# A perceiver layer with 257 context rows: the last column of the probabilities comes to its rows by small DMAs in place of POOL, PE and DVE

## Time and profile before

| | us |
|---|---|
| median of 3 runs | 970.79 (970.17 to 971.96) |
| the profiled execution | 969.11 |
| its span, first to last instruction | 967.1 |
| PE busy | 943.9 |
| DVE busy | 613.0 |
| ACT busy | 607.3 |
| POOL busy | 373.8 |

### The profile page before, as it was taken

One profiled execution on the slowest core, in us unless ns is written; L12 is line 12 of the kernel. 1 busy time (PEld: TensorE's weight loads), 2 busy tenths in 40 slices (PEclk: granted clock), 3 DMA queues, 4 the chain that ended last, 5 costly groups with the idle time before them and its releaser, 6 DMA issues.

```text
span 967.1 us, 23520 instructions
## 1 busy us (share of the span) xinstructions
PE 943.9 (98%) x9012; PEld 783.6 (81%) x9012; DVE 613.0 (63%) x1286; ACT 607.3 (63%) x1487; POOL 373.8 (39%) x484
## 2 busy tenths in 40 slices
PE   9999999999999999999999999999999999999998
PEld 7767888787888878798887878888787888877775
DVE  4765858476685847668485666747567584746461
ACT  3545657667575766767576675757757566674533
POOL 1423534244352524435253352524326252433330
PEclk9999999999999999999999999999999999999999
DMA  8314231322323132132222313122222313222000
GB/s 304 120 51 124 59 105 49 100 81 65 105 78 90 51 101 81 60 110 61 88 69 87 95 60 94 60 87 89 81 80 81 90 49 89 87 73 72 9 12 22
DMA packets 58013, 79.03 MB, mean 82 GB/s; under 512 B 10288, under 2 KB 39856, under 8 KB 57904
## 3 DMA queue, kind: packets, MB, share of 16 engines
q1 hardware_dynamic: 56192, 76.38, 25.9%
q10 hardware_dynamic: 1712, 1.16, 0.4%
HBM read 73.05 MB, written 4.46 MB: 80 GB/s over the span
## 4 chain that ended last, share of the span: by engine, by line
PE 78%; DVE 9%; ACT 7%; issue 3%; POOL 1%; DMA 0%; DVEq 0%; POOLq 0%; ACTq 0%
PE gb L369 16%; PE scores L428 7%; PE acc L459 7%; PE gb L492 6%; PE acc L455 6%; PE scores L432 6%; PE ptp L442 5%; PE acc L460 5%; PE gb L613 3%; PE gb L602 3%; DVE xn L840 3%; ACT probs L685 3%; PE gb L401 3%; DVE probs L853 2%; DVE small L846 2%
## 5 line engine op out<-in xcount | busy, mean ns | idle before, releaser
L1100 POOL TENSOR_TENSOR t_l<-raw_t,t_h 128x516 fp32r<-128x516 f32 x128 | 167.5, 1309 | 193.6 <-PE scores L432 131.0
L685 ACT ACTIVATE probs<-scores,small 128x257 f32<-128x257 f32 x256 | 119.1, 471 | 134.6 <-DVE small L846 134.4
L846 DVE TENSOR_REDUCE small<-scores 128x2 f32<-128x514 f32 x128 | 88.3, 690 | 127.5 <-PE scores L432 127.4
L1109 POOL TENSOR_TENSOR ptm<-probs,head 128x32 f32<-128x32 f32 x128 | 35.1, 274 | 261.9 <-DVE probs L853 261.9
L853 DVE TENSOR_TENSOR probs<-probs,small 128x514 f32<-128x514 f32 x128 | 101.7, 794 | 4.4
L459 PE MATMUL acc<-pt,raw_n 128*128 128x256 f32 x256 | 89.6, 431 | 0.0
L442 PE MATMUL ptp<-ident,probs 128*128 128x128 f32 x512 | 78.7, 276 | 10.5 <-DVE probs L853 9.4
L696 ACT ACTIVATE pt<-ptp 128x512 f32<-128x512 f32 x128 | 77.2, 603 | 13.2 <-PE ptp L442 11.7
L455 PE MATMUL acc<-pt,raw_n 128*64 128x128 f32 x1024 | 82.7, 282 | 2.3 <-ACT pt L696 0.4
L428 PE MATMUL scores<-t_h,qk_h 128*128 128x258 f32 x256 | 83.3, 325 | 0.0
L455 PEld LDWEIGHTS acc<-pt,raw_n 128*64 128x64 f32 x1024 | 55.4, 136 | 31.9 <-issue 21.0
(11 more groups left out here) (178 smaller groups left out, 2768.8 us busy)
## 6 DMA issues: line engine op xcount, KB each, us to landing
raw_t<-in_ctx_t SPq DMA_DIRECT2D x128, 258.0 KB, 3.3
raw_n<-in_ctx_n SPq DMA_DIRECT2D x128, 192.0 KB, 2.4
xb<-in_x SPq DMA_DIRECT2D x16, 256.0 KB, 4.3
vsp<-tail_values SPq DMA_DIRECT2D x256, 2.0 KB
out<-ob SPq DMA_DIRECT2D x16, 256.0 KB, 2.9
xin<-in_x SPq DMA_DIRECT2D x15, 256.0 KB, 2.9
khat<-in_wq ACTq DMA_DIRECT2D x1, 512.0 KB, 4.3
wv<-in_wv SPq DMA_DIRECT2D x1, 512.0 KB, 6.3
```

The lines of the kernel that those rows point to most:

```text
L685: go(probs[n % 2][:, r, 0:L], scores[:, r, 0:L], ACT.Exp, bias=nmax[:, r:r + 1], accum_out=rsum[:, r:r + 1]).then_inc(s["exp_ready"], 1)
L846: v_.tensor_reduce(nmax[:], scores[:, :, 0:L], AX.X, ALU.max, negate=True)\
L1100: p_.tensor_tensor(t_l[m % 2][:], raw_t[m % RING][:], t_h[m % 2][:].bitcast(F32), ALU.subtract)\
```

## The change

The last column is copied by SP. For every batch two DMAs, one for each r, read one element from each of 128 partitions of `probs` and write 4 rows of 32 elements of `psp`, straight to the place where WV needs them. `psp` becomes two buffers, zeroed at the start by DVE (one more memset; the zeros of the second also feed PE's warm-up in place of ones). POOL's tail_column, PE's TP, DVE's psp item, `ptm` and the three tables with their loads are dropped. ACT's exponentials wait for the tail DMAs of n - 2, WV for those of all 8 batches. The values of the last row are loaded only into the half that is read: 8 DMAs a group and not 16. The new copy stands in SP's order at the head of each step, before load_t and load_n.

```diff
-         ["TP"]]
+         []]
...
-        ptm = [sb(f"ptm{i}", [P, 2, 2, G, H]) for i in range(2)]
-        psp = sb("psp", [P, G, S])
-        ones = psp[:].rearrange("p b s -> p (b s)")
+        psp = [sb(f"psp{i}", [P, G, S]) for i in range(2)]
+        zeros = psp[1][:].rearrange("p b s -> p (b s)")
...
                 for h in range(H):
                     cols = slice(h * DH, (h + 1) * DH)
-                    for half in range(2):
-                        sp.dma_start(vsp[half * 64 + h:half * 64 + 64:H, cols], scratch[g * G:(g + 1) * G, cols])\
-                            .then_inc(vsp_in, 16)
+                    half = h // 4
+                    sp.dma_start(vsp[half * 64 + h:half * 64 + 64:H, cols], scratch[g * G:(g + 1) * G, cols])\
+                        .then_inc(vsp_in, 16)
+
+            def tail_column(n):
+
+                g, b = n // G, n % G
+                if n == 0:
+                    sp.wait_ge(s["psp_ready"], 1)
+                sp.wait_ge(s["probs_ready"], n + 1)
+                if b == 0 and g > 1:
+                    bank, k = BANK["WV1", g - 2]
+                    sp.wait_ge(bank_filled[bank], k)
+                for r in range(2):
+                    row = 64 * r + H * b + 4 * r
+                    sp.dma_start(psp[g % 2][row:row + 4, b], probs[n % 2][:, r, L - 1:L]).then_inc(tail_in[n % 2], 16)
...
                     n = i * G + b
+                    if n < B:
+                        tail_column(n)
                     if n + RING + 1 < B:
                         load_t(n + RING + 1)
...
-                drained("TP", g)
-                pe.wait_ge(vsp_in, 256 * (g + 1))
+                for t_in in tail_in:
+                    pe.wait_ge(t_in, 16 * G * (g + 1))
+                pe.wait_ge(vsp_in, 128 * (g + 1))
...
                 if n > 1:
-                    act.wait_ge(s["ptm_ready"], n - 1)
+                    act.wait_ge(tail_in[n % 2], 32 * (n // 2))
...
-            GAPS = [[["psp-1"], ["S2-2", "S3-2"], ["WV0-1", "WV1-1"]],
+            GAPS = [[[], ["S2-2", "S3-2"], ["WV0-1", "WV1-1"]],
...
-            v_.memset(ones, 1.0).then_inc(s["ones_ready"], 1)
+            v_.memset(zeros, 0.0)
+            v_.memset(psp[0][:], 0.0).then_inc(s["psp_ready"], 1)
...
                     part(i, b, 0)
-                    if 0 <= n + 1 < B:
-                        tail_column(n + 1)
                     part(i, b, 1)
```

More of the change, by code:

```diff
@@ L65 @@
 TILES.update({"Sp": ["S0", "S1"], "Sq": ["S2", "S3"], "St": ["St0", "St1"]})
-SHIFT = {"XT": PREP, "TP": HERE}
+SHIFT = {"XT": PREP}
 SHIFT.update({f"q{p}": PREP for p in range(4)})
@@ L166, in build @@
         mask = sb("mask", [P, P], U8)
-        head = sb("head", [P, 2, 2, H])
-        same = sb("same", [P, G])
-        diag = sb("diag", [P, S])
         raw_t = [sb(f"raw_t{i}", [P, 2, LP]) for i in range(RING)]
@@ L250, in build @@
                              "out_done"))
+        tail_in = [sem(f"tail_in{i}") for i in range(2)]
         ctxt_in = [sem(f"ctxt_in{i}") for i in range(RING)]
@@ L254, in build @@
         bank_drained = [sem(f"bank_drained{i}") for i in range(BANKS)]
-        names = ("half_ready ones_ready zeros_ready small_ready scores_ready nmax_ready exp_ready probs_ready pt_ready ptev_ready "
-                 "acc_ready pc_ready ptm_ready var0_ready var1_ready var2_ready rstd0_ready rstd1_ready rstd2_ready xn0_ready xn1_ready xn2_ready high_act_ready high_pool_ready low_ready qk_h_ready xb_ready ob_ready "
+        names = ("half_ready psp_ready zeros_ready small_ready scores_ready nmax_ready exp_ready probs_ready pt_ready ptev_ready "
+                 "acc_ready pc_ready var0_ready var1_ready var2_ready rstd0_ready rstd1_ready rstd2_ready xn0_ready xn1_ready xn2_ready high_act_ready high_pool_ready low_ready qk_h_ready xb_ready ob_ready "
                  "wq_ready weights_ready wz_h_ready xt1_h_ready xt2_h_ready xt2_l_ready o_h_ready o2_h_ready tanh_ready dec_ready hat_ready rhat_ready dve_chain").split()
@@ L263, in build @@
         scratch = nc.dram_tensor("tail_values", [B, INNER], F32, kind="Internal").ap()
-        SMALL = [(mask_raw, a["mask"]), (bw_raw, a["bw"]), (head[:], a["head"]), (same[:], a["same"]),
-                 (diag[:], a["diag"]), (vecs[:, 0:2], a["ln_g"]), (vecs[:, 2:4], a["ln_b"]),
+        SMALL = [(mask_raw, a["mask"]), (bw_raw, a["bw"]),
+                 (vecs[:, 0:2], a["ln_g"]), (vecs[:, 2:4], a["ln_b"]),
                  (vecs[:, 6:14], a["b1"])]
@@ L477, in wz_product @@
                 done("WZ", 0, last)
[L479 to L485, removed]
             def wv(g):
@@ L501, in wv @@
                         rows_ = slice(64 * (h // 4), 64 * (h // 4) + 64)
-                        head(h, vsp[rows_, h * DH:(h + 1) * DH], psp[rows_].rearrange("p b s -> p (b s)"), start=i == 1)
+                        head(h, vsp[rows_, h * DH:(h + 1) * DH], psp[g % 2][rows_].rearrange("p b s -> p (b s)"), start=i == 1)
                     for h in pairs[i]:
@@ L623, in _ @@
             steps = {"WV": wv, "Y1": y1, "v": v, "O2": o2_, "Y2": y2, "Pf": pf_, "Qf": qf_, "Y3": y3,
-                     "TP": turn_tails, "VT": lambda g: tail_values(), "WZ": lambda g: wz_product()}
+                     "VT": lambda g: tail_values(), "WZ": lambda g: wz_product()}
             for n in ("XT", "XT2", "XT3"):
@@ L641, in stay_busy @@
                 for k in range(count):
-                    mm(ptp[:, 0], ones[:, 0:P], ones, start=True, stop=True)
-            pe.wait_ge(s["ones_ready"], 1)
+                    mm(ptp[:, 0], zeros[:, 0:P], zeros, start=True, stop=True)
+            pe.wait_ge(s["psp_ready"], 1)
             stay_busy(WARM)
@@ L705, in step @@
             def step(name, g):
-                if name in ("Y1", "Y2", "Y3", "TP", "Sp", "Sq"):
+                if name in ("Y1", "Y2", "Y3", "Sp", "Sq"):
                     return
@@ L922, in step @@
                     drain(n, g, v_.tensor_tensor(wz_l[:], t[:], wz_h[:].bitcast(F32), ALU.subtract))
[L923 to L927, removed]
                 elif n == "Y1":
@@ L1005, in _ @@
                     [[], ["S0-1", "S1-1"], ["xn0+2"]]]
-            AT_END = [[[["psp-1"], ["S2-2", "S3-2"], ["WV0-1", "WV1-1"]],
+            AT_END = [[[[], ["S2-2", "S3-2"], ["WV0-1", "WV1-1"]],
                        [[], [], ["Y1-1"]],
@@ L1101, in parts @@
                     .then_inc(s["low_ready"], 1)
[L1103 to L1111, removed]
             def hat(n, g):
@@ L1244 @@
     p = np.arange(P)
-    heads = 4 * np.arange(2)[None, :] + p[:, None] // S
-    head = np.repeat((heads[:, :, None] == np.arange(H))[:, :, None], 2, 2).astype(np.float32)
-    same = ((p[:, None] % 64) // H == np.arange(G)).astype(np.float32)
-    diag = (p[:, None] % S == np.arange(S)).astype(np.float32)
     def column(v):
@@ L1257 @@
         "x": np.ascontiguousarray(np.asarray(x).reshape(B * S, D)), "ctx_t": ctx_t, "ctx_n": ctx_n,
-        "ctx_tail": ctx_tail, "head": np.ascontiguousarray(head), "same": same, "diag": diag,
+        "ctx_tail": ctx_tail,
         "wq": chunks(np.asarray(L0_xattn_Wq)), "wk": wk, "wv": wv, "wo": chunks(np.asarray(L0_xattn_Wo)),
```

## The result

The changed kernel takes 991.37 us (median, 991.05 to 992.08), 1.0212 times as long as the kernel before (970.71 in the same comparison; 95% interval of the ratio 1.0194 to 1.023). That is 20.7 us slower, outside the range of 965.5 to 978.0. The sign was that of the forecast, the size was 4.6 times as large.

What follows compares the result with a forecast made beforehand. PE was taken to bound the kernel, with DVE's chain through the second LayerNorm setting the pace at batch 3. Terms -4.8 + 4.5 + 4.8 = +4.5 us on the median 970.8 gave 975.3 us, range 965.5 to 978.

Steps and rivals of the forecast that it cites:

- The sign: Whole kernel: slower, by a sum of +4.5 us; chance of slower 0.44.
- Elsewhere: POOL's earlier operations at batches 0, 4 and 7: the products have room (batch 4's over 2 us), so nothing added.
- TP: PE's stream: four instructions a group dropped, 0.37 us each group in 13 groups, -4.8 us.
- Batch 3: POOL's cast gets between xn1's two halves on DVE, delaying PE 0.30 us in 15 groups, +4.5 us.
- rival 2: DVE keeps its turn at xn1 and wins at batch 6; only TP's gain stays, 966.0 us; chance 0.17.
- Batch 6: POOL's k2 issues before DVE's product at line 853, delaying PE 0.34 us in 14 groups, +4.8 us.
- rival 1: Only batch 3 is hit, the product wins at batch 6: 970.5 us; chance 0.30.
- SP and the traffic: SP's queue and DMA engines: tail DMAs land in time, 32768 element packets at 71 ns have room; 0.
- Rival 4: SP: a tail DMA holds SP for 1.4 us, delaying the next group's exponentials; 977 to 982 us; chance 0.05.

Runs made afterwards that it cites:

- e1: The changed kernel with POOL's wait for the product kept where the tail column stood, the operation itself still dropped: 964.5 us, ratio 0.9933 to the kernel before.
- e3: The changed kernel with POOL's wait for the product in step b = 3 alone: 970.46 us, ratio 0.9999 to the kernel before.
- e12: e9 with two unused tensors, so that tensors allocated behind them lie at the addresses of the kernel before: 958.74 us, ratio 0.9884 to the kernel before.
- e5: The changed kernel with POOL's wait for the product in step b = 2 alone: 984.88 us, ratio 1.015 to the kernel before.
- e6: The changed kernel with POOL's wait for the product in step b = 5 alone: 988.78 us, ratio 1.018 to the kernel before.
- e8: e1 with 16 vsp DMAs a group again and not 8: 1001.94 us, ratio 1.0324 to the kernel before.
- e11: The changed kernel, POOL's t_l of batch 8g + 4 waiting for xn1 and cast of batch 8g + 6 for xn2: 958.61 us, ratio 0.9867 to before.
- e9: e1 with one wait more, POOL's t_l of batch 8g + 4 starting only when xn1 is written: 954.79 us, ratio 0.9842 to the kernel before.
- e2: The kernel before with POOL's tail column moved one step later, no small DMAs, TP kept: 980.16 us, ratio 1.0099 to the kernel before.

## Why the prediction was wrong

**The step that failed** is "*Elsewhere* there is room: ... batch 4's meets a t_l, but its product was ready over 2 us early". It asked whether POOL's earlier operations delay the product of batch 4, and whether PE's transposes feel that. They hardly do: in the changed kernel these transposes wait for 0.1 us in 13 groups together. But it didn't ask what else stands on DVE before that product (both halves of xn2), what stands behind it (Qa0's drain), and which tile of PE's needs the bank. And it saw one operation of POOL there, where three come: the cast in front of t_l meets line 912, and with the tail column gone xb follows t_l at once. That place costs 1.42 us a group against before and 1.46 against e1; times 15 groups 22 us, and e3 takes back 20.9.

The other terms, by their own steps:

- *TP, -4.8 us at 0.37 a group:* step 7 is 0.37 shorter than before, and in e12, at the old addresses, 0.36. Right. The product of the next group's batch 0 now takes 1.75 us, and its slack fell from 1.8 to 0.39 us, against some 0.3 foretold.
- *Batch 3, +4.5 at 0.30:* step 2 is 6.97 before and 7.27 after. Right. xn1's pair took 1.94 us in the place of 1.64, with the cast in between, as worked out:

```profile
490.24 1.30 POOL L1102 TENSOR_TENSOR t_l<-raw_t,t_h 128x516 fp32r<-128x516 f32 x1
491.49 0.68 POOL L1098 CAST t_h<-raw_t 128x516 fp32r<-128x516 f32 x1
...
490.38 1.94 DVE L846 TENSOR_SCALAR xn<-x,mv,rstd 128x256 f32<-128x256 f32 x2 [0.28 <-POOL rstd L1165]
```

  This rules out rival 2, by which DVE would keep its turn. Held back in e5, the cast gives back more than that, 6.2 us, since step 3 gets 0.11 us shorter as well. Why it does was not tried.
- *Batch 6, +4.8 at 0.34:* k2 did come first, by 0.01 to 0.02 us in 15 of the 16 groups, so rival 1 falls too. Step 5 lost 0.35, but step 6 gave 0.16 back: before, PE stood still there ahead of batch 6's product with the context (line 455, 1.6 us in all in groups 3 to 15, worked out from the gaps in PE's trace; 1.48 in e6), and after the change it doesn't. Net 3.1 us (1.0212 - 1.018). The order of two starts that are 0.01 us apart:

```profile
514.40 0.74 POOL L1126 TENSOR_TENSOR khat<-ke,itot 128x256 f32<-128x256 f32 x1
...
514.41 1.28 DVE L859 TENSOR_TENSOR probs<-probs,small 128x514 f32<-128x514 f32 x1
```

  The rule of the Trainium skill that the prediction leaned on here ("SBUF — State Buffer", Who interferes with whom: the one that issues first holds the ports for its whole instruction) agrees with this row.
- *SP and the traffic, 0:* a pair of tail DMAs held SP for 1.14 to 1.57 us, 1.2 having been taken. The exponentials waited for one once, 1.3 us in all. q1 has 31744 packets more than before, which is 32768 single elements less 1024 rows of vsp, so the Trainium skill's one descriptor for each element ("DMA: Bandwidth & Descriptors", Rules for kernel authors) agrees with the count. But they were cheap: 28.5% of 16 x 990.3 us less 25.9% of 16 x 967.1 is 508 us, 16 ns for each new packet and not 71. Rival 4 didn't come, and e8 shows how near it was: the exponentials of the next group's first batch began 3.55 us after the tail DMAs of batch 6 had been issued (median), and in e8, where they waited for them, 1.50 us after.
- *Not foreseen:* the shorter pace of the split products, about -4 us.

The sum with the measured sizes: -5 (14 x 0.36) + 4.5 + 3.1 + 21.9 - 4 = +20.5, against 20.7 measured. Without batch 4 and the addresses, it is +2.6, where the prediction had +4.5. So its own terms carry the sign, and an eighth of the size.

Why the other time of batch 4 was missed can be read in the kernel before: POOL's wait for line 853 is listed there with 261.9 us, and I followed it to the operations behind it at batches 3 and 6 only. At batch 4 I compared the new time of one instruction with its nearest consumer and stopped.

## What to carry to other kernels

A wait on an engine whose operations shut out another's can be worth more than the work that it waits to do: before such a wait is dropped, list for each of its places every operation that it held back, every operation of the other engine that these then meet, and whatever stands behind those in that engine's order, down to the buffers that they free. If work goes and its wait protected something, keep the wait: here a wait at one place took back as much as had been lost (e3), and two waits chosen for the purpose made the kernel 1.3% faster than the one before (e11; with nine, 1.6%, e9). An expensive queue should be costed at its busiest place and not by its mean: SP had some 2 us to spare in one batch of eight (3.55 less 1.50), and the 4.7 us of e8 used them up.

## What the runs showed of the hardware

- DVE's two products of xn, 0.40 us each alone, stand back to back in its order. One POOL operation that had begun before them made 1.70 us of their 0.72; where a second one waited behind it, it got in between the two products, in 14 of 14 groups (2.66 to 2.70 us, the changed kernel's xn2).
- An operation of 0.29 us of POOL's between two longer ones was enough for DVE to get its turn (e2, step 2, 15 of 15 groups). That this is by its timing alone was not tried by itself.
- The pace of matmuls of the same shape and type depends on where their operands lie in SBUF: 114.3 against 118.0 ns with most tensors moved by 1312 bytes a partition (those from the contexts to `pc` by 288), 4 us in 955. Which tensor and which address matter, was not tried.
- A DMA of 128 single elements between two places of SBUF holds SP's queue for 0.56 us (median of 256), about as one of 8 rows of 256 bytes does (4.75 us for eight).
